# A token mixer's front reordered: group 0 first, groups 2 and 3 inside the first steps

## What is computed

```python
xn = _layernorm(x, ln_gamma, ln_beta)
x_unit = _l2norm(xn, axis=-1)
mu_unit = _l2norm(mu, axis=0)
logits = einsum('bnd,des->bnes', x_unit * scale, mu_unit)
dispatch = softmax(logits, axis=1)                 # over tokens
combine = softmax(logits over (e, s), axis=-1)     # over slots
slot_in = einsum('bnd,bnes->besd', xn, dispatch)
h = gelu(einsum('besd,edh->besh', slot_in, w1) + b1)
slot_out = einsum('besh,ehd->besd', h, w2) + b2
out = einsum('besd,bnes->bnd', slot_out, combine)
```

## Time and profile before

| | |
|---|---|
| median of 3 runs | 977.78 us (976.91 to 978.07) |
| profiled execution | 977.11 us, its span 975.4 us |
| busy in the span | PE 78%, PEld 52%, DVE 65%, ACT 54%, POOL 43% |
| first mixer: last additions of the expert layer end, first logits start | 371.4, 384.8 us |
| second mixer: last addition of attention ends, first logits start | 854.4, 872.2 us |

### The profile page before, as it was taken

The page is one execution under the profiler, slowest core; times in us unless marked ns, Lnnn a source line. Parts: engine busy times, 40 slices in busy tenths (PEclk is TensorE's granted clock), DMA queues, the critical chain, the costliest instruction groups (busy, mean ns, idle before and its releaser), DMA issues.

```text
span 975.4 us, 18027 instructions
## 1 busy us (share of the span) xinstructions
PE 764.3 (78%) x5550; PEld 507.5 (52%) x5550; DVE 633.9 (65%) x2291; ACT 523.8 (54%) x1435; POOL 419.5 (43%) x537
## 2 busy tenths in 40 slices
PE   3789992987699902997929788888988999729977
PEld 3679991646599901775813233333333433317757
DVE  4555546685744469554797577777877885585534
ACT  4435542424255418665201576866767777687650
POOL 2046751301467524110376658668576533261100
PEclk9999995995699965999965699989989999859999
DMA  6741113002111130000044324122242200000002
GB/s 158 218 109 48 52 42 91 1 22 65 30 49 52 42 92 1 1 1 1 8 59 55 45 35 62 29 46 44 30 63 32 38 3 4 1 1 1 1 2 87
DMA packets 52526, 41.99 MB, mean 43 GB/s; under 512 B 9224, under 2 KB 48080, under 8 KB 52432
## 3 DMA queue, kind: packets, MB, share of 16 engines
q1 hardware_dynamic: 46784, 31.74, 16.4%
q0 software_dynamic: 4096, 8.40, 2.9%
q10 hardware_dynamic: 1552, 0.70, 0.3%
HBM read 17.35 MB, written 10.49 MB: 29 GB/s over the span
## 4 chain that ended last, share of the span: by engine, by line
PE 54%; DVE 15%; ACT 9%; POOL 7%; issue 7%; DMA 3%; SPq 2%; ACTq 1%; DVEq 0%; POOLq 0%
PE psum L814 8%; PE psum L827 7%; PE psum L1525 5%; PE psum L1296 3%; PE psum L1259 3%; PE psum L768 3%; PE psum L1268 3%; DVE cst L1592 3%; PE psum L1510 2%; DVE half_stats L447 2%; DVE x L717 2%; PE psum L1359 2%; PE psum L1465 2%; PE psum L1497 2%; ACT arena L1654 2%
## 5 line engine op out<-in xcount | busy, mean ns | idle before, releaser
L1592 DVE CUSTOM_DVE_ANT_0 cst<-psum,rot 128x512 bf16<-128x512 f32 (+3 forms) x512 | 219.3, 487 | 67.0 <-PE psum L1497 58.1
L1654 ACT ACTIVATE arena<-psum 128x512 f32<-128x512 f32 (+1 forms) x384 | 178.4, 530 | 54.2 <-PE psum L1510 48.7
L1497 PE MATMUL psum<-arena 48*128 48x512 bf16 (+3 forms) x512 | 121.3, 329 | 17.7 <-DVE row_max L1592 10.9
L1510 PE MATMUL psum<-arena 51*128 51x512 bf16 (+3 forms) x512 | 114.4, 314 | 11.5 <-ACT arena L1654 6.9
L740 ACT ACTIVATE arena<-psum,gate_b1T 128x128 f32<-128x128 f32 x234 | 68.8, 365 | 74.7 <-PE psum L814 74.7
L853 POOL DMA_INDIRECT arena<-xhat_rows,token_of x64 | 61.8, 966 | 104.5 <-DVE token_of L658 81.0
L1749 POOL TENSOR_SCALAR_AFFINE_SELECT arena<-arena 128x384 f32<-128x384 f32 x128 | 63.6, 521 | 96.1 <-ACT arena L1654 96.1
L1525 PE MATMUL psum<-arena 128*32 128x512 f32 (+3 forms) x1024 | 98.3, 482 | 6.7 <-POOL arena L1752 6.7
L814 PE MATMUL psum<-arena 128*128 x624 | 87.8, 286 | 4.9 <-issue 2.8
L827 PE MATMUL psum<-arena 128*128 x624 | 86.7, 282 | 0.5 <-ACT arena L740 0.5
L814 PEld LDWEIGHTS psum<-arena 128*128 128x128 f32 x624 | 78.9, 199 | 9.8 <-issue 9.6
(11 more groups left out here) (249 smaller groups left out, 1636.9 us busy)
## 6 DMA issues: line engine op xcount, KB each, us to landing
arena<-cut SPq DMA_DIRECT2D x192, 64.0 KB
xhat_rows<-xh SPq DMA_DIRECT2D x16, 256.0 KB, 2.3
arena<-result_rows SPq DMA_DIRECT2D x8, 512.0 KB, 6.0
x<-in_L_attn_x SPq DMA_DIRECT2D x4, 512.0 KB, 7.7
arena<-in_L_ffn_w SPq DMA_DIRECT2D x1, 2048.0 KB, 9.5
out<-x SPq DMA_DIRECT2D x4, 512.0 KB, 3.2
arena<-xhat_rows,token_of POOLq DMA_INDIRECT x64, 2.5
result_rows<-arena,token_of POOLq DMA_INDIRECT x64
```

The source lines that it names most:

```text
L1497: mm = pe.matmul(to[:, col:col + (k + 1) * P], q_stack[b % STACKS][rows, h, k * P:k * P + P], k_stack[b % STACKS][rows, h, 0:(k + 1) * P], ...
L1510: mm = pe.matmul(bank[MAX_BANKS + number % EXP_BANKS][:, col:col + S - k * P], k_stack[b % STACKS][rows, h, k * P:k * P + P], q_stack[b % ...
L1592: last = nc.vector.tensor_tensor_reduce(masked_scores[:, number % 2, col:col + n_keys], frm[:, col:col + n_keys], mask[:, S - n_keys:], 1. ...
L1654: nc.scalar.activation(prob_e[g % 2][:, j, first:last], bank[MAX_BANKS + number % EXP_BANKS][:, 0:last - first], ACT.Exp, scale=DH ** -0.5 ...
```

## The change

For group 0 and 1 the order is drawn together, and what groups 2 and 3 need is moved behind the first logits.

- **Centring.** In the first mixer, groups 0 and 1 keep six tiles on ACT and two on DVE; groups 2 and 3 are centred wholly on DVE. In the second mixer all 32 tiles are centred on DVE.
- **DVE, before the steps.** A new `take_last` puts the unit of group 0 and the beta of group 1 in front of the statistics of group 3. Then come the unit of group 1, the scale and shift of group 2 and its centring, and the first maxima.
- **DVE, in the steps.** Beta of group 2 behind the maxima of step 0; scale, shift and centring of group 3 between steps 0 and 1; beta of group 3 in step 1; the units of groups 2 and 3 at once in step 2.
- **ACT.** The square root of the squares is split off as `roots`. Squares and roots of groups 0 and 1 come before the copy of batch 0, squares of group 2 between steps 0 and 1, squares of group 3 and one root for both groups between steps 1 and 2, that is, between exponentials.
- **POOL.** Gamma of group 2 behind the unit rows of batch 2, gamma of group 3 behind those of batch 3.
- **Attention, last bodies.** The statistics of groups 0 to 2 are taken as before, with scale, shift and centring of group 0 between those of groups 1 and 2; scale, shift and centring of group 1 and the beta of group 0 come in the next body, before the last addition.

```diff
@@ expert layer, vector
+                    if g == GROUPS - 1 and n + 1 in last_take:
+                        last_take[n + 1](dve)
+                    else:
+                        stats_after(dve, n + 1, g)
@@ mixer
+        def by_act_of(n):
+            return (BY_ACT, BY_ACT, 0, 0) if stages[n - 1] == "f" else (0, 0, 0, 0)
+
...
             def front_vector(dve, g):
                 centre_vector(dve, g)
-                if between and g >= 1:
-                    shift_vector(g - 1)
-                if between and g >= 2:
-                    unit_vector(g - 2)
+                if g == 1:
+                    shift_vector(0)
+
+            def take_last(dve):
+                stats_chain.engine = dve
+                if between:
+                    unit_vector(0)
+                    shift_vector(1)
+                else:
+                    shift_vector(1)
+                    unit_vector(0)
+                stats_take(dve, n, GROUPS - 1)
@@ mixer, vector
-                if between:
-                    shift_vector(GROUPS - 1)
-                    unit_vector(GROUPS - 2)
-                    unit_vector(GROUPS - 1)
-                else:
-                    shift_vector(0)
-                    shift_vector(1)
-                    unit_vector(0)
-                    shift_vector(2)
-                    unit_vector(1)
-                    shift_vector(3)
-                    unit_vector(2)
-                    unit_vector(3)
+                unit_vector(1)
+                stats_finish(dve, n, 2)
...
-                def step(b, h):
+                def step(b, h, shifted=None, units=None):
                     keep_c(b)
                     max_c(b + 1)
                     keep_d(b, h)
                     max_d(b + 1)
+                    if shifted is not None:
+                        shift_vector(shifted)
+                    if units is not None:
+                        unit_vector(units, 2)
                     keep_in(b)
...
-                step(0, 0)
-                for i in range(3):
+                step(0, 0, 2)
+                stats_finish(dve, n, 3)
+                stats_chain.engine = dve
+                step(1, 1, 3)
+                step(2, 0, None, 2)
+                for i in range(1, 3):
@@ mixer, gpsimd
                 scaled(0)
                 scaled(1)
+                units(0)
+                units(1)
+                units(2)
                 scaled(2)
-                units(0)
+                units(3)
                 scaled(3)
-                for b in range(1, B):
+                for b in range(4, B):
                     units(b)
@@ mixer, scalar
                 stats_root(act, n, 0)
                 stats_root(act, n, 1)
-                centre(0)
+                if between:
+                    centre(0)
+                    centre(1)
                 stats_root(act, n, 2)
-                centre(1)
-                if between:
-                    squares(0)
+                squares(0)
+                roots(0)
+                squares(1)
+                roots(1)
+                copy_xT(0, 0)
                 stats_root(act, n, 3)
-                centre(2)
-                if between:
-                    squares(1)
-                centre(3)
-                if not between:
-                    squares(0)
-                    squares(1)
-                squares(2)
-                copy_xT(0, 0)
-                squares(3)
                 exp_c(0, 0)
                 exp_d(0, 0)
                 step(0, 0)
-                for i in range(3):
+                squares(2)
+                step(1, 1)
+                squares(3)
+                roots(2, 2)
+                step(2, 0)
+                for i in range(1, 3):
@@ attention, vector
                         if (i, hh) == (B, 9):
                             for g in range(GROUPS - 1):
-                                stats_after(dve, n + 1, g)
+                                stats_take(dve, n + 1, g)
+                                if g == 1:
+                                    stats_finish(dve, n + 1, 0)
+                        if (i, hh) == (B + 1, 7):
+                            stats_finish(dve, n + 1, 1)
...
-                stats_after(dve, n + 1, GROUPS - 1)
+                last_take[n + 1](dve)
```

More of the change, by code:

```diff
@@ L432, in build @@
         after_finish = {}
+        last_take = {}
         first_batch = {}
@@ L958, in build @@
         BY_ACT = 6
-        MIX_COUNTS = dict(v=0, centered=GROUPS * BY_ACT, centered_v=GROUPS * (GT - BY_ACT), scaled=B, xn=B, squared=T, norm_sqrt=GROUPS, unit_ready=GROUPS, unit=B, turned=T,
+        MIX_COUNTS = dict(v=0, centered=0, centered_v=0, scaled=B, xn=B, squared=T, norm_sqrt=GROUPS, unit_ready=GROUPS, unit=B, turned=T,
                           xT_ready=B, logit_c=2 * B, logit_d=2 * B, max_c=2 * B, max_d=2 * B, exp_c=T, exp_d=2 * B,
@@ L964, in build @@
         mix_sems = {k: sem(f"m_{k}") for k in MIX_COUNTS}
+        def by_act_of(n):
+            return (BY_ACT, BY_ACT, 0, 0) if stages[n - 1] == "f" else (0, 0, 0, 0)
         def mix(n):
             s, at = mix_sems, {k: v * stages[:n].count("m") for k, v in MIX_COUNTS.items()}
+            between = stages[n - 1] == "f"
+            by_act = by_act_of(n)
+            for k in range(n):
+                if stages[k] == "m":
+                    at["centered"] += sum(by_act_of(k))
+                    at["centered_v"] += T - sum(by_act_of(k))
             def centre_vector(dve, g):
                 dve.wait_ge(ready_sem, GROUPS * n + g + 1)
-                for t in range(GT * g + BY_ACT, GT * g + GT):
+                for t in range(GT * g + by_act[g], GT * g + GT):
                     nc.vector.tensor_scalar(xn[:, t, :], x[:, t, :], mean[:, t:t + 1], rstd[:, t:t + 1],
@@ L978, in shift_vector, with unit_vector @@
                     nc.vector.tensor_tensor(tiles, tiles, beta[:].unsqueeze(1).to_broadcast([P, TB, D]), ALU.add).then_inc(s["xn"], 1)
-            def unit_vector(g):
+            def unit_vector(g, groups=1):
                 norm, unit = st[:, 3, :], st[:, 4, :]
-                c = slice(GT * g, GT * g + GT)
-                nc.vector.wait_ge(s["norm_sqrt"], at["norm_sqrt"] + g + 1)
+                c = slice(GT * g, GT * (g + groups))
+                nc.vector.wait_ge(s["norm_sqrt"], at["norm_sqrt"] + g + groups)
                 stats_chain(nc.vector.tensor_scalar(norm[:, c], st[:, 2, c], 1e-12, None, ALU.max))
                 stats_chain(nc.vector.reciprocal(unit[:, c], norm[:, c]))
-                nc.vector.tensor_scalar(unit[:, c], unit[:, c], mscale[:, 0:1], None, ALU.mult).then_inc(s["unit_ready"], 1)
-            between = stages[n - 1] == "f"
+                nc.vector.tensor_scalar(unit[:, c], unit[:, c], mscale[:, 0:1], None, ALU.mult).then_inc(s["unit_ready"], groups)
             def front_vector(dve, g):
                 centre_vector(dve, g)
-                if between and g >= 1:
-                    shift_vector(g - 1)
-                if between and g >= 2:
-                    unit_vector(g - 2)
+                if g == 1:
[9 more added lines that the diff above has]
+                stats_take(dve, n, GROUPS - 1)
             after_finish[n] = front_vector
+            last_take[n] = take_last
             def vector(dve):
@@ L1150, in centre @@
                     act.wait_ge(ready_sem, GROUPS * n + g + 1)
-                    for t in range(GT * g, GT * g + BY_ACT):
+                    for t in range(GT * g, GT * g + by_act[g]):
                         nc.scalar.activation(xn[:, t, :], x[:, t, :], ACT.Identity, bias=shift_by[:, t:t + 1],
@@ L1162, in squares, with roots @@
                         nc.scalar.activation(square[:, t % GT, :], xn[:, t, :], ACT.Square, accum_out=st[:, 5, t:t + 1]).then_inc(s["squared"], 1)
-                    act.wait_ge(s["squared"], at["squared"] + GT * g + GT)
-                    c = slice(GT * g, GT * g + GT)
-                    nc.scalar.activation(st[:, 2, c], st[:, 5, c], ACT.Sqrt).then_inc(s["norm_sqrt"], 1)
+                def roots(g, groups=1):
+                    act.wait_ge(s["squared"], at["squared"] + GT * (g + groups))
+                    c = slice(GT * g, GT * (g + groups))
+                    nc.scalar.activation(st[:, 2, c], st[:, 5, c], ACT.Sqrt).then_inc(s["norm_sqrt"], groups)
                 def copy_xT(b, h):
```

11 lines of the change are left out of this document (6 added, 5 removed).

## The result

The changed kernel takes 970.53 us (median of 5 runs, 969.41 to 972.78) where the kernel before takes 977.78 in the runs beside it: a ratio of 0.993, with a 95% interval of [0.991, 0.995]. The profiled execution took 971.89 us with a span of 970.1, against 977.11 and 975.4 before.

What follows compares the result with a forecast made beforehand. Fronts were taken as bound by DVE and ACT, steps by TensorE. Gains of 4.6 us in each mixer less 1.2 for the lock gave 8.0 less: 977.78 to 969.8 us, range 965.5 to 975.3.

Steps and rivals of the forecast that it cites:

- First logits of the first mixer: First mixer, front: logits of batch 0 start at 376.2 instead of 384.82, 8.6 us earlier.
- Logits of batch 1: First mixer, front: logits of batch 1 start about 385.5 instead of 393.56, 8.0 us earlier.
- Steps of the first mixer: First mixer, logits of batch 1 to batch 4: stalls from the moved work give back 3.4 us.
- Attention's end: Before the second mixer: six more centrings on DVE and delayed small sums make attention end about 2.2 us later.
- Second front: Second mixer: logits of batch 1 start 8.4 us earlier, less 0.4 for transposes at the lower clock.
- The port lock: POOL's gamma amid DVE's centring chains at five places: bounds 0 and 6.2 us, one place lost taken, 1.2.
- the case is nearer the first (POOL comes mid-chain): Centring chains: POOL's gamma mostly waits and DVE loses nothing, so only one place of five, 1.2 us, is counted.
- My first rival: Lock goes POOL's way at all five places, exponentials late: 6.2 us lost, 974.8; chance 0.15.
- rival 2: ACT: a table switch holds longer than its row, or Square brings loads: 5.1 us, 974.9; chance 0.1.
- rival 3: Step 2 stall: TensorE's clock falls to 1.2 GHz for over a step, up to 8 us more, 985.8; chance 0.05.

Runs made afterwards that it cites:

- first: New order in the first mixer only, the second mixer and attention's end in the old order; ratio 0.9969 to the kernel before.
- second: New order in the second mixer and the end of attention before it only, first mixer old; ratio 0.9973 to the kernel before.
- fourth: Changed kernel with POOL's gamma waiting until all eight tiles of a group are centred; ratio 0.9932 to the kernel before.
- fifth: Changed kernel with ACT centring six tiles each of groups 0 and 1 at attention's end; ratio 0.9911 to the kernel before.
- sixth: Changed kernel with ACT's root of group 2 moved behind its last copy of an attention result; ratio 0.991 to the kernel before.
- tenth experiment: The fifth, with POOL's gamma of group 0 also waiting for the variance of group 2; ratio 0.9898 to the kernel before.
- ninth: Group 0 still first, but the work on groups 2 and 3 done before batch 0's maxima and exponentials; ratio 1.0113 to the kernel before.
- third: Changed kernel with the square root of groups 2 and 3 replaced by a copy, so no table switch in the steps; ratio 0.9913 to the kernel before.
- seventh: Changed kernel with DVE making the reciprocal root of groups 2 and 3 by Newton steps, without ACT's root; ratio 0.9917 to the kernel before.
- eighth: Changed kernel with the changes of the fourth, fifth, sixth and seventh together; ratio 0.9846 to the kernel before.
- eleventh: The eighth, with POOL's gamma of group 0 also waiting for the variance of group 2; ratio 0.9854 to the kernel before.
- twelfth: The eleventh, with the Newton units made per group, each in its own step before DVE's weights copy; ratio 0.9856 to the kernel before.

## Why the prediction was nearly right, step by step

The direction, the mechanism and the size hold: 7.25 less, 8.0 forecast, 970.53 inside the range. Against the rows the terms stand so:

- **First logits of the first mixer**: 8.6 earlier forecast, 8.77 measured (26.97 after A instead of 35.74). **Logits of batch 1**: 8.0 forecast, 7.70 measured. The centring chain at 378.85 took 3.09 instead of 2.16, and with the gamma held back batch 1 came 0.95 earlier, so without the lock this term would have been above its forecast. 1.07 of it depends on the clock in the profile of the kernel before, as said above.
- **Steps of the first mixer**: 3.4 back forecast, 4.19 measured. Mis-sized. The stalls that the steps named are all there: the copy of batch 3 waits 1.66 (1.95 forecast), the transposes of batch 4 wait 0.75 for POOL's unit (0.5 forecast), and slots_in waits 0.62 in step 1, where 0.25 was forecast. The last of these stands behind a centring chain of 3.1 that delays the maxima. With batch 2 (0.56, forecast 0.6) the four waits are 3.59 in sum, where 3.3 was forecast; the rest lies behind them, in a term that the forecast had at nothing. After a wait TensorE's next group starts about 0.16 later than the idle time says: slots_in of step 1 starts 2.50 after the d logits, and 1.72 after them in the kernel before, with 0.62 of idle. (The kernel before needs 24.57 by its timeline; the 24.74 of the prediction are by the chain's rows.) Net 3.51 instead of 4.6; the mixer alone measured 3.0.
- **Attention's end**: +2.2 forecast, +3.58 measured (16.95 instead of 13.37). Also mis-sized, in three parts. The root of group 2 starts 8.03 after the load instead of 5.49: 2.54, where the forecast has 2.3. It had 1.56 of centrings and 0.5 for small sums beside POOL; the centrings cost 2.52 (3.12 instead of 0.60), and the small sums of group 2 took 0.17 each, as before. The transposes at 847.19, begun 5.02 after TensorE last worked, take 1.94 instead of 1.14. DVE starts on their first half, so that 0.53 of the 0.8 reaches the product (it starts 4.70 after them instead of 4.17), where I had 0.4 (and counted it elsewhere). The last 0.53 I had as a risk of up to 1.2 and counted at nothing: DVE is still in its beta when the product is there. The timeline of DVE in the changed kernel shows it, against a product that ends at 853.97 (851.89 and 2.08):

```profile
846.15 0.17 DVE L462 TENSOR_SCALAR st<-st 128x8 f32<-128x8 f32 x1
...
853.41 1.28 DVE L991 TENSOR_TENSOR arena<-arena,beta 128x512 f32<-128x512 f32 x2
854.61 0.67 DVE L1640 TENSOR_TENSOR x<-x,psum 128x512 f32<-128x512 f32 x1
```

- **Second front**: logits of batch 1 come 7.78 earlier over both intervals (11.36 less 3.58), where 8.0 was forecast after the 0.4. The extra loss in attention's end was thus met by a front shorter than I had counted: 5.24 from E to b0, where I had 6.25 (856.6 to 862.85).
- **The port lock**: one place of five at 1.2 forecast. In the trace every chain of centrings that POOL's gamma meets pays 0.95, and it is inside the terms above. The sentence that failed is "the case is nearer the first (POOL comes mid-chain)": to come mid-chain is what makes DVE pay. The row that it leaned on (4.58) was misread as well: POOL waited there beside four betas, not beside centrings, and in the changed kernel too a gamma waits out a chain of betas (853.57). The other row, 4.13 for eight additions, was the one that carried over. My first rival's mechanism was the real one; its size, 6.2, was not reached, since 0.95 is less than the 1.25 I took and part of it lies beside other waits.
- **The table**: rival 2, a longer hold at each switch or a load for Square, did not come. The rows above show 1.28 and none, and the switch's removal gives 1.28 a mixer.
- **The clock**: rival 3 came in a small form. In the second mixer of the profiled execution, after the stall of 1.66, the level fell and eight logits took 3.47 instead of 1.99. It cost 1.7 and not 8, since the clock was back within the step: from b4 on the logits take 1.89 again. Over the profiles of the changed kernel and of the first, second, fourth, fifth, sixth and tenth experiment, twelve mixers hold a stall of 1.65 to 2.15 before batch 3. In four of them the logits behind it took 3.47 to 3.63, in a fifth 2.45, in the other seven 1.99. The ninth, with its stall of 12.90, is left out. In the third, seventh, eighth, eleventh and twelfth no stall in the steps is longer than 1.05, and in none of their ten mixers did the level fall. The changed kernel's spread over its runs, 969.41 to 972.78, is about two such falls wide; that they cause it is argued and not shown.

In sum: each mixer was forecast at 4.6 and brought 3.5 and 3.6, 2.1 less together; the allowance of 1.2 for the lock covers over half of that. The rest, 0.9, is about the 0.75 by which the forecast was too good. So part of the closeness is luck: the allowance was made for one lost place, and what it covers is the sum of a lock at six places, the waits in the steps and attention's end, less a second front that was shorter than counted.

## What to carry to other kernels

Between two operations that POOL and DVE both have to do, look at which is in mid-chain when the other becomes ready, and at which instruction it meets: here a gamma got in among centrings in all six chains and each paid one whole gamma, while beside betas it waited for the last of them in the two places above. A row of one kind does not price the other. Before work is moved behind a waiting instruction on an in-order engine, list what already waits there: a root of 0.21 us in front of a copy cost 2 us here, and to swap the two was one line. And where work is moved out of a front into steps that are bound by another engine, its price is the stalls that are left between them: here 4.2 of 7.7 us, and with the table switch, the lock and the order of two instructions mended, 2.5 of 8.7.

## What the runs showed of the hardware that I had not expected

- A POOL instruction over 128x512 that becomes ready among queued DVE centrings makes one of these take up to 1.32 instead of 0.34 us, and sums of 128x8 take 0.90 and 1.23 instead of 0.17. Beside a chain of DVE betas it is POOL that waits: a gamma took 2.25 beside two (changed kernel, 853.57) and 3.36 beside four (kernel before, the first of the two in the earlier trace rows), instead of 1.26, so both sides can lose.
- A TensorE stall of 1.65 to 2.15 us between dense stretches was followed by slower logits (3.47 to 3.63 us for eight, once 2.45, instead of 1.99) in five cases of twelve, and in seven it was not.
- Square runs under Exp's table with no load, 0.30 each; a load is 1.28 and the activation behind it starts 0.01 to 0.02 after it ends.
